# Graph attention heads: the destination row stays in two adjacent PSUM banks, the relus read it there, and its products stand in front of the last turned tile

## The reference, cut to what matters

```
h = x @ W                                  # (625, c) for this head
a_src = (h * att_src).sum(-1)              # one number per node
a_dst = (h * att_dst).sum(-1)
e = leaky_relu(a_src[src] + a_dst[dst], 0.2)        # one number per edge
m = segment_max(e, dst);  p = exp(e - m[dst])
s = segment_sum(p, dst);  alpha = p / (s[dst] + eps)
out = segment_sum(alpha * h[src], dst) + b
```

## Time and profile before

| | |
|---|---|
| median of 3 runs | 3021.53 us (3019.8 to 3021.64) |
| the profiled execution's own time | 3015.4 us |
| its span | 3013.6 us |
| TensorE matmul busy | 2735.0 us, 91% |
| VectorE busy | 1418.9 us, 47% |
| ScalarE busy | 1117.7 us, 37% |
| mean granted TensorE clock | 0.963 |

### The profile page before, as it was taken

The page is one execution under the profiler, slowest core; times in us unless marked ns, Lnnn a source line. Parts: engine busy times, 40 slices in busy tenths (PEclk is TensorE's granted clock), DMA queues, the critical chain, the costliest instruction groups (busy, mean ns, idle before and its releaser), DMA issues. The chain is left out here.

```text
span 3013.6 us, 48711 instructions
## 1 busy us (share of the span) xinstructions
PE 2735.0 (91%) x20003; PEld 2488.3 (83%) x20003; DVE 1418.9 (47%) x3609; ACT 1117.7 (37%) x2085; POOL 705.8 (23%) x260
## 2 busy tenths in 40 slices
PE   8999999997669999998999899989987899997697
PEld 8999999994339878998879899988677888894597
DVE  8777565573131235478623532323735545005632
ACT  6632265551013113249322433233634234453131
POOL 0134311110002312310425143324023231112121
PEclk9999999998889999999999999999998999999799
DMA  2022221108962112220212122211001121110121
GB/s 68 12 77 74 85 69 38 54 21 315 415 278 67 48 33 64 74 85 1 71 41 74 43 77 75 80 54 59 1 17 55 52 69 59 35 32 2 32 64 58
DMA packets 163790, 220.37 MB, mean 73 GB/s; under 512 B 21521, under 2 KB 142795, under 8 KB 163570
## 3 DMA queue, kind: packets, MB, share of 16 engines
q1 hardware_dynamic: 163570, 217.26, 21.6%
HBM read 215.31 MB, written 1.92 MB: 72 GB/s over the span
## 5 line engine op out<-in xcount | busy, mean ns | idle before, releaser
L58 PE MATMUL ps<-weights_r,buf_r 128*125 128x256 f32 (+3 forms) x4080 | 548.5, 286 | 21.7 <-DVE buf_r L3238 7.6
L58 PEld LDWEIGHTS ps<-weights_r,buf_r 128*125 128x125 f32 (+1 forms) x4080 | 516.8, 188 | 25.9 <-issue 14.6
L268 POOL TENSOR_TENSOR weights_r<-weights,head_weights_r 128x1536 fp32r<-128x1536 f32 (+1 forms) x78 | 274.4, 3518 | 1121.0 <-ACT head_weights_r L261 1121.0
L268 POOL TENSOR_TENSOR weights_r<-weights,weights_r 128x1536 fp32r<-128x1536 f32 (+1 forms) x79 | 273.4, 3461 | 1036.5 <-ACT weights_r L261 1036.5
L58 PE MATMUL ps<-xT_r,weights_r 128*128 128x376 f32 (+1 forms) x2100 | 346.5, 310 | 0.0
L58 PE MATMUL ps<-head_weights_r,buf_r 128*125 128x256 f32 (+2 forms) x2400 | 329.1, 283 | 0.0
L58 PEld LDWEIGHTS ps<-xT_r,weights_r 128*128 128x128 f32 x2100 | 314.8, 189 | 4.6 <-issue 2.4
L58 PEld LDWEIGHTS ps<-head_weights_r,buf_r 128*125 128x125 f32 x2400 | 305.5, 187 | 0.0
L58 PE MATMUL ps<-weights_r,xT_r 128*125 128x256 f32 x1680 | 233.2, 283 | 7.6 <-issue 5.9
L261 ACT ACTIVATE head_weights_r<-weights 128x1536 fp32r<-128x1536 f32 (+1 forms) x78 | 114.3, 1466 | 331.8 <-PE ps L58 207.5
L58 PEld LDWEIGHTS ps<-weights_r,xT_r 128*125 128x125 f32 x1680 | 213.6, 187 | 9.6 <-issue 6.5
(11 more groups left out here) (359 smaller groups left out, 4240.0 us busy)
## 6 DMA issues: line engine op xcount, KB each, us to landing
expert_regions<-in_L_ffn_w SPq DMA_DIRECT2D x64, 576.0 KB, 15.0
expert_regions<-in_L_ffn_w SPq DMA_DIRECT2D x48, 768.0 KB, 20.5
weights<-in_L_mix_fc_w SPq DMA_DIRECT2D x24, 768.0 KB, 4.4
weights<-in_L_gnn_W SPq DMA_DIRECT2D x18, 768.0 KB, 4.6
weights<-in_L_ffn_W SPq DMA_DIRECT2D x12, 768.0 KB, 4.7
weights<-in_L_mix_w_mapT SPq DMA_DIRECT2D x9, 768.0 KB, 4.8
weights<-in_L_gnn_W_out SPq DMA_DIRECT2D x9, 768.0 KB, 4.6
weights<-in_L_mix_kqv_wT SPq DMA_DIRECT2D x9, 768.0 KB, 4.5
```

Of the source, the lines that this page charges most:

```text
L58: mm = net.nc.tensor.matmul(ps, net.r(stationary(s, k)), net.r(moving(m, k)), start=(n == 0 and k == 0), stop=(stop and n == 2 and k == kc ...
L268: self.nc.gpsimd.tensor_tensor(self.r(load.dst), load.dst, self.r(load.high), ALU.subtract).then_inc(self.low_made, 1)
```

## The change

The change does four things. ScalarE's two copies of row are gone, and with them the buffer: `leaky` reads the row in PSUM. For that, the two groups of a row are written to two adjacent banks (an even one and the next; a bank of the ring is skipped where the next one is odd), the first piece at the end of its bank and the second at the start of the next, so that 625 numbers lie side by side. Both banks stay taken until the last `leaky` of the head. The row of head k+1 is made in the step that applies head k, and no longer one step earlier. And in TensorE's list it stands in front of the last of the ten turned groups, where before the row (of head k+2) stood behind it.

```diff
     def step(self, k, scores, apply):
         pe, act, dve = (self.order[e] for e in ("pe", "act", "dve"))
         n = k + 1
-        ahead = n + 1 < len(self.heads)
         if k < 0:
             pe += [("row", n, j) for j in range(2)]
-            act += [("row", n, j) for j in range(2)]
         if apply:
             turns = [("turn", k, s, j) for j in range(2) for s in range(NT)]
-            pe += turns
+            pe += turns[:-1] + ([("row", n, j) for j in range(2)] if scores else []) + turns[-1:]
             act += [q for q in turns if self.turn_engine(*q[2:]) == "act"]
             dve += [q for q in turns if self.turn_engine(*q[2:]) == "dve"]
-        if scores and ahead:
-            pe += [("row", n + 1, j) for j in range(2)]
         if apply:
             pe += [("apply", k, t, j) for t in range(NT) for j in range(self.nw)]
...
                 if t + 1 < NT:
                     act.append(("leaky", n, t + 1))
-                elif ahead:
-                    act += [("row", n + 1, j) for j in range(2)]
                 act.append(("exp", n, t))
...
+    def banks(self):
+
+        net, bank = self.net, {}
+        for q in self.order["pe"]:
+            if q[0] == "row" and q[2] == 0 and net.nbank % 2:
+                b = net.bank()
+                net.freed[b] = net.freed[b - BANKS]
+            b = bank[q] = net.bank()
+            engine, entry = self.reader(q)
+            net.freed[b] = ({"act": net.act, "dve": net.dve}[engine].sem, self.at[engine][entry])
+        return bank
+
+    def row(self, n, j=None):
+
+        b, w = self.bank["row", n, 0] % BANKS, (HALVES[0][1] - HALVES[0][0]) * TP
+        t0, t1 = HALVES[j] if j is not None else (0, NT)
+        return self.net.ps[:TP, b:b + 2, :].rearrange("p b c -> p (b c)")[:, 512 - w + t0 * TP:512 - w + t1 * TP]
+
     def reader(self, q):
-        return {"row": ("act", q), "turn": (self.turn_engine(*q[2:]) if q[0] == "turn" else "", q), "apply": ("dve", ("out",) + q[1:])}[q[0]]
+        return {"row": ("act", ("leaky", q[1], NT - 1)), "turn": (self.turn_engine(*q[2:]) if q[0] == "turn" else "", q), "apply": ("dve", ("out",) + q[1:])}[q[0]]
...
-            if q[0] == "row":
-                t0, t1 = HALVES[q[2]]
-                self.wait(act, "pe", *q)
-                if k > 0 and q[2] == 0:
-                    self.wait(act, "act", "leaky", k - 1, NT - 1)
-                ins = nc.scalar.activation(self.net.asb[:TP, t0 * TP:t1 * TP], self.ps(q, TP, (t1 - t0) * TP), ACT.Identity)
...
             elif q[0] == "leaky":
                 t = q[2]
                 if t == 0:
-                    self.wait(act, "act", "row", k, 1)
+                    self.wait(act, "pe", "row", k, 1)
...
-                ins = nc.scalar.activation(self.P[k % 2][:, t], self.net.asb[:TP, :], ACT.Prelu, bias=self.heads[k][1][:, t:t + 1], scale=-SLOPE, alpha=1.0 / SLOPE)
+                ins = nc.scalar.activation(self.P[k % 2][:, t], self.row(k), ACT.Prelu, bias=self.heads[k][1][:, t:t + 1], scale=-SLOPE, alpha=1.0 / SLOPE)
```

More of the change, by code:

```diff
@@ L1875, in tensor @@
                 t0, t1 = HALVES[q[2]]
-                ps = self.ps(q, TP, (t1 - t0) * TP)
+                ps = self.row(k, q[2])
                 for t in range(t0, t1):
@@ L1899, in scalar @@
             k = q[1]
-            if q[0] == "row":
-                t0, t1 = HALVES[q[2]]
-                self.wait(act, "pe", *q)
-                if k > 0 and q[2] == 0:
-                    self.wait(act, "act", "leaky", k - 1, NT - 1)
-                ins = nc.scalar.activation(self.net.asb[:TP, t0 * TP:t1 * TP], self.ps(q, TP, (t1 - t0) * TP), ACT.Identity)
-            elif q[0] == "turn":
+            if q[0] == "turn":
                 t0, t1 = HALVES[q[3]]
```

## The result

The changed kernel takes 3033.92 us (median of 9 runs, 3027.83 to 3038.26), the kernel before beside it 3021.64 us (9 runs, 3013.66 to 3025.36). The ratio is 1.0040, with a 95% interval of 1.0028 to 1.0052: 12.3 us slower, or between some 8 and 16. The forecast was 3033.2 us.

What follows compares the result with a forecast made beforehand. TensorE bounds layer 0's groups, a ring of waits layer 2's heads. Terms 7.61 + 8.76 - 4.36 - 0.3 = +11.7 us on 3015.4 give 3027.1, with the 6.1 us offset 3033.2 us; range 3027 to 3038.

Steps and rivals of the forecast that it cites:

- the first stages: Four first stages make one row in place of two before a dense product: -1.09 us each, -4.36 us.
- The products that move: Row products, 1.09 us, now delay the last transposes and leaky: +7.61 us in layer 2, +8.76 in layer 0.
- The ring: Layer 2's cycle of waits from leaky to next leaky, through VectorE and turned tiles: from 11.45 to 12.54 us.
- the steps: Passage-by-passage terms of layer 2's heads: first +1.07 us, next four +4.36, sixth +2.18, last 0.
- The rule on order: TensorE's matmuls complete in program order, so no transpose passes the row products; otherwise the ring stays at 11.45 us.
- The copies that go: ScalarE's two row copies, 0.72 us, lie in a gap; the last exp waits 0.90 us, not 0.18: worth 0.
- Rival 3: ScalarE's row copies were on the ring after all, so 8.6 us come off: 3024.6 us, chance 0.07.
- The relus: ScalarE's relus reading PSUM take 782 ns, not 805; only a head's first counts, 16 passages: -0.3 us.
- Rival 1: The first stages give nothing back, something other than TensorE ending them: +16.1 us, 3037.6 us, chance 0.08.
- rival 2: Held banks stall TensorE at the next head's first turned tile: up to +10 us, 3043 us, chance 0.03.
- Rival 4: Faster: ScalarE is late at the last tile, leaky doesn't move, copies come off: -9.7 us, 3011.8 us, chance 0.04.

Runs made afterwards that it cites:

- order_only: The kernel before with only TensorE's row products moved in front of the step's last turned tile: 3038.11 us, 1.0066 of the kernel before.
- rows_doubled: The changed kernel with each row product issued twice: 3058.93 us, 1.0138 of the kernel before.
- rows_behind: The changed kernel with the row products behind the last turned tile of the same step: 3025.72 us, 1.0022 of the kernel before.
- leaky_early: The kernel before with the next head's first leaky between the copies of the two halves of turned tiles: 3014.48 us, 0.9987 of the kernel before.
- copied_early: The kernel before with the next head's first leaky and first max ahead of all copies of turned tiles: 3010.47 us, 0.9968 of the kernel before.
- rows_first: The changed kernel with the row products before the first turned tile, other groups using the six banks left: 3027.98 us, 1.0034 of the kernel before.
- psum_early: rows_first with copied_early's early leaky and max, and one more bank skipped before the second half: 3021.04 us, 1.0005 of the kernel before.
- ring_end: The changed kernel, skipping a bank only where the row's pair would wrap round the ring's end: 3031.68 us, 1.0038 of the kernel before.

## Why the prediction was right

**The size.** The sum, +11.7 us, stands against 12.3 in the medians and 12.1 in the stretches that the change touches. The interval of the medians, 8 to 16 us, is too wide to tell more, and in the stretches misses cancel: the passages came 0.6 us under the forecast, a wait for a bank that it hadn't put at 0.90, and the first stages agree by luck (below).

**The products that move.** Right, and by its own mechanism. The ring is 12.51 us where 12.54 was forecast, layer 0's passages 12.83, 12.83 and 11.75 for 12.86, 12.86 and 11.77. The first and the sixth passage of layer 2 lost about what the steps said, +0.98 and +2.14 for +1.07 and +2.18. The relu behind the copy of the last tile starts 0.48 us behind the applies, forecast 0.47. order_only shows that the order costs this with all else as before, and rows_doubled that each passage with a row pays all of its products' duration. rows_behind adds what the prediction's words didn't separate: its chain, last tile behind the products and relu behind that tile's copy, is the one that the changed kernel waits in, but with the products behind the tile 0.79 of the 1.06 us would still be lost, because the row is made in the step that uses it.

**The rule on order.** TensorE's matmuls ran in program order here: each last pair of transposes starts when the products are through (1376.75), none slipped past. So by that rule of the Trainium skill's page "PSUM — Partial Sum Buffer", section "Engine vs sequencer instructions", the trace agrees; a queue that let it pass would have left 11.45 us.

**The copies that go.** Right: the last exp waits 0.90 us as forecast, and layer 0's first passage is 12.86 us with them and 12.83 without. Rival 3 is out.

**The relus.** 773 ns, not 782, so they save 0.03 us each. Only the first of a head counts, and the passages lie 0.02 to 0.04 us under their forecast: the size of that term.

**The first stages.** Rival 1 is out: they gave -4.57 us for -4.36. But only two of the four terms agree. The other two miss in opposite directions, and that the sum agrees is luck. Layer 0's second group and layer 2 gave -1.10 and -1.12 us, as forecast. The first group gave -2.86, and TensorE's timelines of before and of after show where:

```profile
420.01 4.60 PE L1805 MATMUL ps<-ident,buf 125*125 125x125 f32 x25 [2.01 <-DVE stats L842]
```

```profile
419.98 2.75 PE L1805 MATMUL ps<-ident,buf 125*125 125x125 f32 x23 [2.00 <-DVE stats L842]
```

The group's first turned tiles ran at a granted clock of 0.62 before and at 1.00 after, 1.6 us that the forecast's term left out. This is not one execution's chance. In all five profiled kernels whose first stage has 20 row passes (before, order_only, leaky_early, copied_early, rows_doubled) these transposes took 4.38 to 4.60 us at 0.60 to 0.62, in all five with 10 passes they ran at 1.00. Why the clock goes with passes that lie some 37 us ahead, no run shows. The prediction had also read that TensorE's idle times in these stretches show nothing larger than 1.04 us; the 2.01 us above is larger. It stands behind the dense product, and the kernel after has it too (2.00), so it moved with the product and does not by itself explain the slow transposes.

The third group went the other way, in this execution alone:

```profile
565.17 2.33 PE L1890 MATMUL ps<-ident,stats 125*125 125x125 f32 x10 [0.46 <-DVE buf_r L1355]
```

```profile
566.00:568.00 2.00, 2.00 (x12) 2.00 (x11) 1.75 (x4) 0.71 (x2) 2.00 (x1) 0.50 0.00 0
```

The ten passes took 2.33 us, where the second group's show 1.32. The second row is the busy time from 566 to 568 us, with a granted clock of 0.50, the lower level of 1.2 GHz. So this stage lost 0.51 us where it should have won 1.09. The bank wait of 0.46 us right ahead doesn't explain it: it stands ahead of row products at six places in four kernels (after, rows_doubled, rows_first, psum_early), and only here did they run slow. In ring_end and rows_behind, which don't have that wait, the four stretches come to 6.1 us less than before. That is what this term is worth there, and the forecast had 4.36.

**What was missed.** The prediction weighed the banks only between heads (rival 2), where they cost nothing: the first turned tile waits for the count. It did not follow the ring to the first stage of a group, where the skipped bank makes the row products wait 0.46 us for a reader that they didn't have. It is +0.90 us, shown by ring_end, and too small to move the forecast. Rival 4 is out, since leaky moved by the products' whole time.

## What to carry to other kernels

When several engines are tied in a ring of waits, ask of every moved piece who stands behind it in the order and when its result is first needed. In layer 2 the row products cost the ring nothing where they were made a step ahead and stood behind the tiles, their full 1.09 us in front of the last tile, 0.79 behind it but in the step that uses them, and 0.40 in TensorE's idle time ahead of the first tile. An engine freed of work that lay in its own waiting time gives nothing back, and the row to read is the wait that grows by just that much (0.18 to 0.90 us). The gain lay in letting the next head's first relu and max start ahead of the copies (copied_early, 3010.47 us), which needs a row made before the turned tiles are. A row held in PSUM through them takes two of eight banks from the ring, and in psum_early the waits for banks gave the gain back in every second passage.

## What the hardware showed that I had not expected

Granted clocks under 1.00 turned up inside a ring whose work and waits repeat: in order_only two passages with the same instructions and the same 2.02 us wait had 1.00 and 0.87, and took 12.53 and 13.20 us. Waits of 1.76 us at the same place (the changed kernel) left it at 1.00 throughout layer 2's heads, but in rows_first the last passage, with a wait of 1.77 us there, had 0.86 and took 12.92 us where the others take 11.85. So a lengthened ring can lose time twice, and one profile doesn't say how often.

In layer 0's first group the clock went with the work of a stage some 37 us earlier, in ten kernels out of ten: 0.60 to 0.62 with 20 row passes there, 1.00 with 10. A term for work that is taken out can be larger than its duration, here 2.86 us for 1.09.

And the stretch between layer 0 and layer 2, which no kernel changes, differed by up to 6 us, half of the whole effect. A difference of two spans is no measure of a change of this size; the stretches that it touches, compared one by one over several kernels, say more.
